# Expert weights turned in 32x32 blocks on VectorE and through DRAM, in place of TensorE transposes, with a new order on all engines

## The chip, the cores and the metric

The kernel runs on one core of a Trainium2 chip. A core has TensorE (PE, matrix products), VectorE (DVE), ScalarE (ACT), GpSimd (POOL) and SyncE (SP), which run their own instruction streams and wait for each other by semaphores. Products go from SBUF to the eight banks of PSUM, each 128 partitions by 512 fp32; DMA moves data between DRAM and SBUF and is issued here by SP and POOL. The metric is the time of one execution on the device in microseconds, lower is better.

## The reference

```
x: [8, 2048, 256] fp32, D = 256
x = x + layernorm(attention(layernorm(x)))
x = x + layernorm(ffn(layernorm(x)))

attention: q, k, v = x @ w.T ; sq, sk = elu(q) + 1, elu(k) + 1 ; per chunk of 128 rows
    A = (sq @ sk.T) * causal
    num = A @ v + sq @ S_kv ; den = A.sum(-1) + sq @ z
    S_kv += sk.T @ v ; z += sk.sum(0)          # carried from chunk to chunk of a sequence
    local = num / max(den, eps) ; memory part = (sq @ memory) / max(sq @ memory_norm, eps)
    output = (g * memory part + (1 - g) * local) @ w_o.T

ffn (hidden x, 4 heads, 1024 experts, 8 chosen a head):
    sim of x @ W_q.T with keys -> top 8 of 16 and of 64 keys -> sums of pairs -> top 8 of them
    w = silu((x . down_embed[expert]) * softmax(scores))
    experts = sum over heads and experts of w * up_embed[expert]
    dense = silu(x @ W_up.T) @ W_down.T         # 1024 wide
    out = dense + experts
```

## The kernel before

The 8 x 2048 rows are 128 tiles of 128 rows; tile t is chunk t // 8 of sequence t % 8, so a tile's state comes from the tile 8 earlier. `pipeline(body)` runs 128 + 8 - 1 steps, and in a step each engine's `body` works on several tiles: t[0] is the newest, t[7] the oldest, t[k] being the tile k behind. `if t[k] is not None` leaves out what lies before the first or past the last tile. The order of the instructions in a `body` is written out by hand or by a planner, engine by engine; engines take them strictly in that order, TensorE apart, which may load weights ahead. `steady` marks steps in the middle where some waits are left out since others imply them.

All products are fp32; the trace has two matmul passes for each `matmul`, and one for each transpose. A tile's way is as follows. x_in is loaded (SP, L360) and normalised to xn1, which TensorE turns (L516) into `t_ps`, ScalarE copying it to xn1T. Products give q and k (wqT, wkT into bank 1), v (wvo), then scores (`sig` by `sig`, L511 by `product`), the part of the state, the memory part (mem_x, bank 2), the masked scores by v (L547, bank 3), and the state's addition (L563, into banks 1 and 2, added on VectorE). The result is mixed and normalised on ScalarE, VectorE and GpSimd (power for the reciprocal root, L387) to x_mid, normalised to xn2, and turned on TensorE to xn2T.

The second half is dense over all 1024 experts. `route` gives the key scores, `deT` (two products of 512 columns, banks 6 and 7) the product of x with every down_embed. GpSimd adds every pair of keys for each head (`sums`, L401, 128x1024), VectorE takes maxima (`top`, `best`), masks (`picked`, 128x1024) and multiplies with ScalarE's exponentials (`prob`), and ScalarE's Silu writes the weights of head h to wexp[:, h, :]. Two accumulating DMAs on GpSimd's queue add the four heads: first heads 0 and 2 to 1 and 3 (L441, 1 MB), then 1 to 3 (L409, 512 KB).

The summed weights wexp[:, 3, :] have rows of the tile on the partitions, while the product with `ue` needs experts there. TensorE therefore transposes eight 128x128 blocks into banks 5 and 3 (`g_ps`, L587 and L591), and ScalarE copies each bank to gT (L692, L703). TensorE then adds two chains of eight products into bank 4: wdownT with hT (the dense part; hT is ScalarE's Silu of the wupT products, L647 and L682, in banks 2 and 1), and ue with gT:

```
product(y_ps, IC, lambda c: hT[:, t[6] % 2, c, :], lambda c: wdownT[:, c, :], stop=False)
...
pe.wait_ge(s_expert_weights_T_0_ready, t[6] + 1)
pe.wait_ge(s_expert_weights_T_1_ready, t[6] + 1)
product(y_ps, EC, lambda c: gT[:, t[6] % 2, c, :], lambda c: ue[:, c, :], start=False)
```

ScalarE copies the result, VectorE scales it and adds x_mid (L793), and SP stores it (L355). SP issues nothing else in a step but the load of x_in.

## Time and profile before

| | |
|---|---|
| median of 3 runs | 3050.55 us (3050.07 to 3052.66) |
| profiled execution | 3049.49 us, its span 3047.8 us |
| TensorE busy | 3001.7 us, 98% |
| ScalarE busy | 2622.7 us, 86% |
| VectorE busy | 2169.6 us, 71% |
| GpSimd busy | 1821.7 us, 60% |

The busy share says how much of the span an engine executed something, not whether it set the time. A timeline lists instructions in order of their start, runs of the same kind merged (x8 is eight of them), with the duration from the first start to the last end. Instructions of one engine overlap in their pipelines, so the next row often starts before the row above has ended. A note in square brackets gives idle time ahead of a row and who ended it.

### The profile page before, as it was taken

What the parts mean: (1) busy time and instruction counts of PE and PEld (TensorE: products, weight loads), DVE (VectorE), ACT (ScalarE), POOL (GpSimd) and SP (SyncE); (2) the same over time, 40 slices, a digit from 0 to 9 for tenths busy, and PEclk for the clock granted to TensorE, in tenths of its full rate; (3) what the DMA queues carried; (4) which work ended last, traced back from release to release, by engine and by line L of the source; (5) the groups of instructions that cost most, each with busy time, mean ns of one, the idle gap of its engine ahead of it and who ended that gap; (6) DMA issues with size and microseconds to landing.
All of it is one profiled execution on the core that took longest, in us unless ns stands there. A gap on an engine that the chain in (4) does not pass through costs nothing.

```text
span 3047.8 us, 48454 instructions
## 1 busy us (share of the span) xinstructions
PE 3001.7 (98%) x16426; PEld 2446.1 (80%) x16426; DVE 2169.6 (71%) x5636; ACT 2622.7 (86%) x4106; POOL 1821.7 (60%) x2455
## 2 busy tenths in 40 slices
PE   6999999999999999999999999999999999999997
PEld 5788888888888888888888888888888888888886
DVE  4777777767776777777677767776777777677774
ACT  4988888888888888888888888888888888888985
POOL 2665665566566656655665666566556655665664
PEclk8999999999999999999999999999999999999999
DMA  3443444344334434443444344334434443443443
GB/s 92 81 85 73 81 83 80 77 82 83 75 77 86 81 74 79 85 80 75 81 83 78 77 84 83 74 77 87 81 73 80 83 80 77 81 83 76 82 85 71
DMA packets 96202, 244.17 MB, mean 80 GB/s; under 512 B 8659, under 2 KB 46548, under 8 KB 95956
## 3 DMA queue, kind: packets, MB, share of 16 engines
q0 software_dynamic: 53248, 201.34, 36.7%
q1 hardware_dynamic: 42708, 39.73, 4.4%
q8 instruction: 132, 2.16, 0.3%
q14 instruction: 114, 0.93, 0.1%
HBM read 22.94 MB, written 16.78 MB: 13 GB/s over the span
## 4 chain that ended last, share of the span: by engine, by line
PE 96%; DMA 1%; issue 1%; ACT 0%; POOL 0%; DVE 0%; SPq 0%; POOLq 0%; DVEq 0%
PE banks L511 84%; PE banks L563 3%; PE banks L516 2%; PE banks L547 2%; PE banks L587 2%; PE banks L591 2%; PE banks L550 1%; DMA wexp<-wexp 1%; DMA sums<-in_L_ffn_keys_dram 0%; SPq L345 0%; POOL sums L401 0%; PE banks L502 0%; PE banks L495 0%; PE banks L480 0%; DVE prob L861 0%
## 5 line engine op out<-in xcount | busy, mean ns | idle before, releaser
L401 POOL TENSOR_TENSOR sums<-scores 128x1024 f32<-128x1024 f32 x512 | 1076.6, 2218 | 392.8 <-ACT scores L636 392.8
L511 PEld LDWEIGHTS banks<-xn2T,wupT 128*128 128x128 f32 x4096 | 477.3, 192 | 9.2 <-DVE state L848 2.7
L511 PE MATMUL banks<-deT,xn2T 128*128 128x512 f32 x1024 | 481.3, 592 | 0.0
L511 PE MATMUL banks<-xn2T,wupT 128*128 128x128 f32 x4096 | 478.2, 275 | 1.9 <-DVE state L848 1.9
L511 PE MATMUL banks<-wdownT,hT 128*128 128x256 f32 x2048 | 464.4, 380 | 0.0
L511 PE MATMUL banks<-ue,gT 128*128 128x256 f32 x2048 | 462.9, 379 | 0.0
L511 PEld LDWEIGHTS banks<-wdownT,hT 128*128 128x128 f32 x2048 | 390.1, 191 | 53.7 <-issue 0.5
L511 PEld LDWEIGHTS banks<-ue,gT 128*128 128x128 f32 x2048 | 388.6, 190 | 53.8 <-issue 0.7
L387 POOL TENSOR_TENSOR rstd<-var_eps,minus_half 128x1 f32<-128x1 f32 x512 | 329.9, 704 | 56.3 <-DVE var_eps L829 38.2
L413 POOL TENSOR_TENSOR cprob<-cmask,cdif 128x112 f32<-128x112 f32 x128 | 65.9, 515 | 396.6 <-DVE cmask L751 396.6
L511 PEld LDWEIGHTS banks<-deT,xn2T 128*128 128x128 f32 x1024 | 185.3, 190 | 129.9 <-issue 122.9
L424 POOL TENSOR_TENSOR wexp<-wexp,w_last 128x1 f32<-128x1 f32 x128 | 26.2, 205 | 364.7 <-ACT z_last L696 364.7
L511 PE MATMUL banks<-route,xn2T 128*128 128x512 f32 x512 | 242.2, 596 | 0.7 <-ACT xn2T L700 0.7
L804 DVE SCALAR_TENSOR_TENSOR sig<-banks,rqk 128x512 f32<-128x512 f32 x128 | 88.5, 691 | 193.9 <-ACT banks L642 193.9
L843 DVE SCALAR_TENSOR_TENSOR picked<-sums,cand_best,banks 128x1024 f32<-128x1024 f32 x128 | 163.9, 1280 | 62.0 <-PE banks L511 62.0
L654 ACT COPY sk_nat<-banks 128x256 f32<-128x256 f32 x120 | 44.6, 372 | 176.1 <-PE banks L550 176.1
L820 DVE TENSOR_SCALAR dens<-banks 128x2 f32<-128x2 f32 x128 | 20.5, 160 | 246.6 <-PE banks L547 246.6
L788 DVE SCALAR_TENSOR_TENSOR prob<-picked,rz,prob 128x1024 f32<-128x1024 f32 x128 | 164.5, 1285 | 13.7 <-DVE picked L784 0.5
L682 ACT ACT_TABLE_LOAD x128 | 164.2, 1283 | 2.3
L650 ACT ACT_TABLE_LOAD x127 | 162.9, 1283 | 2.2
L861 DVE SCALAR_TENSOR_TENSOR prob<-picked,rz,prob 128x1024 f32<-128x1024 f32 x128 | 164.3, 1284 | 0.0
L776 DVE SCALAR_TENSOR_TENSOR prob<-picked,rz,prob 128x1024 f32<-128x1024 f32 x128 | 163.9, 1281 | 0.0
(140 smaller groups left out, 7244.3 us busy)
## 6 DMA issues: line engine op xcount, KB each, us to landing
wexp<-wexp POOLq DMA_DIRECT2D x128, 1024.0 KB, 7.9
wexp<-wexp POOLq DMA_DIRECT2D x128, 512.0 KB, 4.7
x_in<-_attn_hidden_states_dram SPq DMA_DIRECT2D x128, 128.0 KB, 2.1
out_dram<-x_out SPq DMA_DIRECT2D x128, 128.0 KB, 1.7
wexp<-in_L_ffn_W_up_dram SPq DMA_DIRECT2D x1, 1024.0 KB, 7.1
prob<-in_L_ffn_down_embed_dram SPq DMA_DIRECT2D x1, 1024.0 KB, 9.6
ue<-in_L_ffn_up_embed_dram SPq DMA_DIRECT2D x1, 1024.0 KB, 12.0
wexp<-in_L_ffn_W_down_dram SPq DMA_DIRECT2D x1, 1024.0 KB, 13.0
```

The costliest lines, as they stand in the source:

```text
L387: return nc.gpsimd.tensor_tensor(rstd[:, n, m:m + 1], var_eps[:, n, m:m + 1], minus_half[:, :], ALU.pow)
L401: return nc.gpsimd.tensor_tensor(sums[:, k, :, :], scores[:, k, 0:XIN].unsqueeze(2).broadcast_to([P, XIN, NKEYS]), scores[:, HEADS + k, :] ...
L413: nc.gpsimd.tensor_tensor(cprob[:, :, :], cmask[:, :, :], cdif[:, :, 0:NCAND], ALU.mult).then_inc(s_cand_prob_ready, 1)
L511: last = nc.tensor.matmul(out, lhs(c), rhs(c), start=(start and c == 0), stop=(stop and c == chunks - 1))
L563: last = nc.tensor.matmul(ds_ps[:, c, :], sk_nat[:, c * P:(c + 1) * P], v_one[:, :], start=True, stop=True)
L650: nc.scalar.activation(cdif[:, :, :], cdif[:, :, :], ACT.Exp).then_inc(s_cand_exp_ready, 1)
L682: nc.scalar.activation(flat(hT[:, t[4] % 2, 4:8, :]), u_ps[1][:, :], ACT.Silu).then_inc(s_hidden_1_ready, 1)
L776: nc.vector.scalar_tensor_tensor(prob[:, 1, :], picked[:, 1, :], rz[:, t[5] % 2, 1:2], prob[:, 1, :], ALU.mult, ALU.mult).then_inc(s_head_ ...
L788: nc.vector.scalar_tensor_tensor(prob[:, 3, :], picked[:, 1, :], rz[:, t[5] % 2, 3:4], prob[:, 3, :], ALU.mult, ALU.mult).then_inc(s_head_ ...
L804: nc.vector.scalar_tensor_tensor(sig[:, t[3] % 2, :, :], eqk, 1.0, rqk[:, :, :], ALU.min, ALU.add).then_inc(s_sigma_ready, 1)
L843: nc.vector.scalar_tensor_tensor(picked[:, 0, :], head(sums, 0), best[:, 0, TOP - 1:TOP], down, ALU.is_ge, ALU.mult).then_inc(s_head_0_sel ...
L861: nc.vector.scalar_tensor_tensor(prob[:, 0, :], picked[:, 0, :], rz[:, t[4] % 2, 0:1], prob[:, 0, :], ALU.mult, ALU.mult).then_inc(s_head_ ...
```

## The change

The transposes on TensorE (L587, L591), their two copies on ScalarE and their four semaphores go. In their place VectorE turns the 32x32 blocks of the summed weights into `w_blocks`, one instruction with a write in steps of 8 elements; SP stores `w_blocks` to the DRAM scratch `w_way` (512 KB, 2 buffers), waits for that store, and issues four loads of 128 KB into gT, one for each quarter of its partitions. gT is now [128, row of the tile, chunk], and the product takes `gT[:, t[7] % 2, :, c]`, whose elements stand 8 apart.

```
-        gT = sb("gT", [P, 2, EC, P])
+        gT = sb("gT", [P, 2, P, EC])
+        w_blocks = sb("w_blocks", [P, EXPERTS])
+        w_way = nc.dram_tensor("w_way", [2, P, EXPERTS], fp32).ap()
-    SLOTS = 4
+    SLOTS = 8
+    MID_SLOTS = 8
-        STAGES = 8
+        STAGES = 10
...
+            def gather(dst, way, s_in):
+                for j in range(BLOCKS):
+                    sp.dma_start(dst[j * BLOCK:(j + 1) * BLOCK, :, :].rearrange("p (i t) c -> p i (t c)", t=BLOCK),
+                                 way.rearrange("(i q) (j n) -> j q i n", q=BLOCK, j=BLOCKS)[j]).then_inc(s_in, 16)
...
+                if t[7] is not None:
+                    sp.wait_ge(s_expert_weights_blocks_turned, t[7] + 1)
+                    sp.dma_start(w_way[t[7] % 2, :, :], w_blocks[:, :]).then_inc(s_expert_weights_blocks_out[t[7] % 2], 16)
+                    moved(sp, s_expert_weights_blocks_out, t[7], 1)
+                    gather(gT[:, t[7] % 2, :, :], w_way[t[7] % 2, :, :], s_expert_weights_blocks_in[t[7] % 2])
...
-                if t[5] is not None:
-                    pe.wait_ge(s_heads_summed, 16 * (t[5] + 1))
-                    for k in range(4):
-                        e = k
-                        last = nc.tensor.transpose(g_ps[0][:, k * P:(k + 1) * P], wexp[:, HEADS - 1, e * P:(e + 1) * P], ident[:, :])
-                    last.then_inc(s_expert_weights_T_0_in_psum, 1)
...
+                if t[7] is not None:
+                    moved(pe, s_expert_weights_blocks_in, t[7], BLOCKS)
+                    product(y_ps, EC, lambda c: gT[:, t[7] % 2, :, c], lambda c: ue[:, c, :], start=False).then_inc(s_y_in_psum, 1)
...
-                if t[5] is not None:
-                    act.wait_ge(s_expert_weights_T_0_in_psum, t[5] + 1)
-                    nc.scalar.copy(flat(gT[:, t[5] % 2, 0:4, :]), g_ps[0][:, :]).then_inc(s_expert_weights_T_0_ready, 1)
...
+            def blocks(x):
+                return x.rearrange("p (c j q) -> p j c q", j=BLOCKS, q=BLOCK)
+            def turned_blocks(x, chunks):
+                return x[:, :].rearrange("p (j t c) -> p j c t", j=BLOCKS, c=chunks)
...
+                if t[7] is not None:
+                    dve.wait_ge(s_heads_summed, 16 * (t[7] + 1))
+                    moved(dve, s_expert_weights_blocks_out, t[7] - 1, 1)
+                    nc.vector.transpose(turned_blocks(w_blocks, EC), blocks(wexp[:, HEADS - 1, :])).then_inc(s_expert_weights_blocks_turned, 1)
```

`moved` waits for the DMAs of tile t on one of two semaphores, by t's parity. x_in and x_mid now have 8 buffers each. The bodies of all engines stand in another order, and most pieces belong to a tile one or two steps older (10 stages). The three places below show it.

TensorE from the products of ue to the turn of xn2 and on to route; before:

```order
L511 MATMUL banks<-ue,gT 128x256 x7
L511 MATMUL banks<-xn2T,wupT 128x128 [waits state_ready]
L511 MATMUL banks<-xn2T,wupT 128x128 x15
L587 MATMUL banks<-ident,wexp 128x128 [waits heads_summed]
L587 MATMUL banks<-ident,wexp 128x128 x3
L591 MATMUL banks<-ident,wexp 128x128 x4
L516 MATMUL banks<-ident,xn 128x128 [waits xn2_ready,xn1T_ready]
L516 MATMUL banks<-ident,xn 128x128
L511 MATMUL banks<-xn1T,wqT 128x128 [waits hidden_1_ready,xn1T_ready]
L511 MATMUL banks<-xn1T,wqT 128x128 x3
L511 MATMUL banks<-xn1T,wkT 128x128 x4
L511 MATMUL banks<-route,xn2T 128x512 [waits xn2T_ready]
```

and with the change:

```order
L529 MATMUL banks<-xn2T,wupT 128x128 [waits state_ready]
L529 MATMUL banks<-xn2T,wupT 128x128 x7
L529 MATMUL banks<-wvo,xn1T 128x256 [waits xn1T_ready]
L529 MATMUL banks<-wvo,xn1T 128x256
L529 MATMUL banks<-xn1T,wqT 128x128 [waits hidden_1_ready]
L529 MATMUL banks<-xn1T,wqT 128x128 x3
L529 MATMUL banks<-xn1T,wkT 128x128 x4
L529 MATMUL banks<-xn2T,wupT 128x128 x8
L529 MATMUL banks<-ue,gT 128x256 [waits expert_weights_blocks_in_0]
L529 MATMUL banks<-ue,gT 128x256 x7
L534 MATMUL banks<-ident,xn 128x128 [waits xn2_ready]
L534 MATMUL banks<-ident,xn 128x128
```

The transposes of wexp are gone. The upper wupT half (into bank 1) now stands only the two wvo products ahead of wqT, which writes bank 1 again and waits for hidden_1_ready, ScalarE's hT.

ScalarE around that hT (table loads are the switches between the exponential and Silu); before, from the exponentials on:

```order
L669 ACTIVATE prob<-sums,neg_max 128x1024 [waits head_2_sums_ready]
L671 ACTIVATE prob<-sums,neg_max 128x1024 [waits head_3_sums_ready]
L676 COPY y_sb<-banks 128x256 [waits y_in_psum]
L679 COPY xn1T<-banks 128x256 [waits xn1T_in_psum]
L682 ACT_TABLE_LOAD
L682 ACTIVATE hT<-banks 128x512 [waits up_1_in_psum]
L685 ACTIVATE wexp<-prob 128x1024 [waits head_0_weighed,head_pairs_summed]
```

and with the change:

```order
L677 ACTIVATE cdif<-cdif 128x144 [waits differences_ready]
L680 ACTIVATE prob<-sums,neg_max 128x1024 [waits neg_max_ready,head_0_sums_ready]
L683 ACTIVATE mix_sq,var_eps<-mix 128x257 [waits mix_ready]
L689 ACTIVATE prob<-sums,neg_max 128x1024 [waits head_1_sums_ready]
L692 COPY xn1T<-banks 128x256 [waits xn1T_in_psum]
L695 ACT_TABLE_LOAD
L695 ACTIVATE hT<-banks 128x512 [waits up_1_in_psum]
L698 COPY v_one<-banks 128x256 [waits v_in_psum]
L701 ACT_TABLE_LOAD
L701 ACTIVATE prob<-sums,neg_max 128x1024 [waits head_3_sums_ready]
```

hT stood between exponentials and a series of Silus; now it is a single Silu between exponentials, with a table load on either side. The table load itself has no wait. A step has four table loads as before.

VectorE ahead of the maxima of the key scores; before:

```order
L780 SCALAR_TENSOR_TENSOR prob<-picked,rz,prob 128x1024 [waits head_2_selected,head_2_prob_ready]
L784 SCALAR_TENSOR_TENSOR picked<-sums,cand_best,banks 128x1024 [waits head_1_weighed,head_3_sums_ready]
L788 SCALAR_TENSOR_TENSOR prob<-picked,rz,prob 128x1024 [waits head_3_selected,head_3_prob_ready]
L793 SCALAR_TENSOR_TENSOR x_out<-y_sb,rstd,x_mid 128x256 [waits y_rstd,x_stored]
L798 MAX top<-scores 128x8 [waits route_scores_ready]
```

and with the change:

```order
L753 TENSOR_SCALAR xn<-x_mid,mv,rstd 128x256 [waits x_mid_rstd]
L769 SCALAR_TENSOR_TENSOR x_out<-y_sb,rstd,x_mid 128x256 [waits y_rstd,x_stored]
L774 SCALAR_TENSOR_TENSOR prob<-picked,rz,prob 128x1024 [waits head_3_selected,head_3_prob_ready]
L778 SCALAR_TENSOR_TENSOR prob<-picked,rz,prob 128x1024 [waits head_2_selected,head_2_prob_ready]
L783 STREAM_TRANSPOSE w_blocks<-wexp 128x4x8x32 [waits expert_weights_blocks_out_1,heads_summed]
L787 MAX top<-scores 128x8 [waits route_scores_ready]
```

The block transpose stands between the last head's product and the first of twelve maxima. It waits for the second accumulating DMA and for the store of the tile before.

## Rows read from the trace of the kernel before

**Rows 1.** The page: busy times, and TensorE's granted clock in 40 slices.

```profile
PE 3001.7 (98%) x16426; PEld 2446.1 (80%) x16426; DVE 2169.6 (71%) x5636; ACT 2622.7 (86%) x4106; POOL 1821.7 (60%) x2455
...
PEclk8999999999999999999999999999999999999999
```

**Rows 2.** PE's waits, the first row: line, releaser, total us, times, longest.

```profile
PE banks L587 <- DMA wexp<-wexp: 13.4, 3, 10.5
```

**Rows 3.** PE's timeline, one step: start, us, line, out<-in, form, count.

```profile
1500.77 0.60 PE L547 MATMUL banks<-v_one,at 128*128 128x258 f32 x2
...
1501.42 1.88 PE L511 MATMUL banks<-deT,xn2T 128*128 128x512 f32 x4
...
1504.23 3.62 PE L511 MATMUL banks<-ue,gT 128*128 128x256 f32 x16
1507.68 3.73 PE L511 MATMUL banks<-xn2T,wupT 128*128 128x128 f32 x32
1511.26 0.60 PE L587 MATMUL banks<-ident,wexp 128*128 128x128 f32 x4
...
1512.13 0.38 PE L516 MATMUL banks<-ident,xn 128*128 128x128 f32 x2
...
1514.13 1.88 PE L511 MATMUL banks<-route,xn2T 128*128 128x512 f32 x4
1515.85 1.03 PE L511 MATMUL banks<-wvo,xn1T 128*128 128x256 f32 x4
1516.72 3.62 PE L511 MATMUL banks<-wdownT,hT 128*128 128x256 f32 x16
...
1524.08 0.60 PE L547 MATMUL banks<-v_one,at 128*128 128x258 f32 x2
```

**Rows 4.** ACT's timeline in that step, same columns, idle time ahead in brackets.

```profile
1501.62 0.37 ACT L654 COPY sk_nat<-banks 128x256 f32<-128x256 f32 x1 [1.50 <-PE banks L550]
...
1505.77 1.14 ACT L671 ACTIVATE prob<-sums,neg_max 128x1024 f32<-128x1024 f32 x1
...
1508.55 1.28 ACT L682 ACT_TABLE_LOAD   x1
1509.84 0.60 ACT L682 ACTIVATE hT<-banks 128x512 f32<-128x512 f32 x1
...
1516.05 0.58 ACT L636 COPY scores<-banks 128x512 f32<-128x512 f32 x1
```

**Rows 5.** Timeline of ACT and PE where PE had waited, near the end.

```profile
2995.71 0.36 ACT L700 COPY xn2T<-banks 128x256 f32<-128x256 f32 x1
...
2996.12 1.98 PE L511 MATMUL banks<-route,xn2T 128*128 128x512 f32 x4 [0.66 <-ACT xn2T L700]
2997.95 3.62 PE L511 MATMUL banks<-wdownT,hT 128*128 128x256 f32 x16
```

**Rows 6.** POOL's timeline in the step of rows 3 and 4.

```profile
1516.71 1.90 POOL L401 TENSOR_TENSOR sums<-scores 128x1024 f32<-128x1024 f32 x1 [3.03 <-ACT scores L636]
1518.58 1.02 POOL L434 TENSOR_TENSOR cand_best<-top 128x64 f32<-128x64 f32 x4
...
1522.20 0.86 POOL L445 TENSOR_TENSOR cdif<-cand_best 128x144 f32<-128x144 f32 x1
1522.59 0.63 POOL L447 TENSOR_TENSOR neg_max<-zero,cand_best 128x4 f32<-128x4 f32 x1
```

**Rows 7.** DVE's timeline, one instruction over 1024 elements.

```profile
1506.79 1.28 DVE L861 SCALAR_TENSOR_TENSOR prob<-picked,rz,prob 128x1024 f32<-128x1024 f32 x1
```

**Rows 8.** DMA issues: out<-in, queue, count, KB each, us from issue to landing.

```profile
wexp<-wexp POOLq DMA_DIRECT2D x128, 1024.0 KB, 7.9
wexp<-wexp POOLq DMA_DIRECT2D x128, 512.0 KB, 4.7
...
out_dram<-x_out SPq DMA_DIRECT2D x128, 128.0 KB, 1.7
```

**Rows 9.** Groups by line: weight loads, busy us and mean ns, then idle.

```profile
L511 PEld LDWEIGHTS banks<-ue,gT 128*128 128x128 f32 x2048 | 388.6, 190 | 53.8 <-issue 0.7 <-ACT mix L656 0.2
```

More of the change, by code:

```diff
@@ L41, in sandwich_kernel @@
     HALF = 512
+    BLOCK = 32
+    BLOCKS = P // BLOCK
     LAST_IN = EXPERTS - 1
@@ L521, in body @@
             def body(t, steady):
+                if t[5] is not None:
+                    product(d_ps[0], DC, lambda c: xn2T[:, t[5] % 2, c, :], lambda c: deT[:, c, 0:HALF]).then_inc(s_down_0_in_psum, 1)
+                if t[4] is not None:
+                    wait(pe, s_sk_ready, t[4] + 1, KEPT)
+                    pe.wait_ge(s_mix_memory_part, t[4] + 1)
+                    if t[4] < KEPT:
+                        for c in range(DC):
+                            last = nc.tensor.matmul(ds_ps[:, c, :], sk_nat[:, c * P:(c + 1) * P], v_one[:, :], start=True, stop=True)
+                        last.then_inc(s_state_add_in_psum, 1)
@@ new lines, in body @@
+                if t[3] is not None:
+                    pe.wait_ge(s_xn1_ready, t[3] + 1)
+                    turn(t_ps, xn1).then_inc(s_xn1T_in_psum, 1)
+                if t[7] is not None:
+                    pe.wait_ge(s_hidden_1_ready, t[7] + 1)
+                    pe.wait_ge(s_hidden_0_ready, t[7] + 1)
+                    if not steady:
+                        wait(pe, s_y_ready, t[7])
+                    product(y_ps, IC, lambda c: hT[:, t[7] % 2, c, :], lambda c: wdownT[:, c, :], stop=False).then_inc(s_y_hidden_in_psum, 1)
@@ new lines, in body @@
+                if t[5] is not None:
+                    wait(pe, s_state_ready, t[5] + 2, KEPT)
+                    for k in range(4):
+                        ic = 4 + k
+                        last = product(u_ps[1][:, k * P:(k + 1) * P], DC, lambda c: wupT[:, c, ic * P:(ic + 1) * P],
+                                       lambda c: xn2T[:, t[5] % 2, c, :])
+                    last.then_inc(s_up_1_in_psum, 1)
+                if t[3] is not None:
+                    pe.wait_ge(s_xn1T_ready, t[3] + 1)
+                    product(v_ps, DC, lambda c: xn1T[:, c, :], lambda c: wvo[:, c, :]).then_inc(s_v_in_psum, 1)
+                    wait(pe, s_hidden_1_ready, t[3] - 1)
+                    if not steady:
+                        wait(pe, s_state_ready, t[3], KEPT)
+                    for side, w in enumerate((wqT, wkT)):
+                        for ec in range(DC):
+                            col = (side * DC + ec) * P
+                            last = product(qk_ps[:, col:col + P], DC, lambda c: w[:, c, ec * P:(ec + 1) * P], lambda c: xn1T[:, c, :])
+                    last.then_inc(s_qk_in_psum, 1)
@@ L593, in body @@
[L593 to L604 removed]
+                    product(d_ps[1], DC, lambda c: xn2T[:, t[4] % 2, c, :], lambda c: deT[:, c, HALF:]).then_inc(s_down_1_in_psum, 1)
@@ new lines, in body @@
+                if t[4] is not None:
+                    wait(act, s_sk_in_psum, t[4] + 1, KEPT)
+                    if t[4] < KEPT:
+                        nc.scalar.copy(sk_nat[:, :], sk_ps).then_inc(s_sk_ready, 1)
+                if t[6] is not None:
+                    act.wait_ge(s_head_3_weighed, t[6] + 1)
+                    wait(act, s_expert_weights_blocks_turned, t[6])
+                    nc.scalar.activation(wexp[:, 3, :], prob[:, 3, :], ACT.Silu).then_inc(s_head_3_weights_ready, 1)
@@ new lines, in body @@
+                if t[5] is not None:
+                    act.wait_ge(s_head_1_sums_ready, t[5] + 1)
+                    if not steady:
+                        wait(act, s_head_1_weights_ready, t[5])
+                    nc.scalar.activation(prob[:, 1, :], head(sums, 1), ACT.Exp, bias=neg_max[:, t[5] % 2, 1:2]).then_inc(s_head_1_prob_ready, 1)
+                if t[3] is not None:
+                    act.wait_ge(s_xn1T_in_psum, t[3] + 1)
+                    nc.scalar.copy(flat(xn1T), t_ps).then_inc(s_xn1T_ready, 1)
@@ L701, in body @@
[L701 to L706 removed]
+                    act.wait_ge(s_head_2_sums_ready, t[5] + 1)
@@ L708, in _ @@
+                    nc.scalar.activation(prob[:, 2, :], head(sums, 2), ACT.Exp, bias=neg_max[:, t[5] % 2, 2:3]).then_inc(s_head_2_prob_ready, 1)
             pipeline(body)
@@ L790, in body @@
[L790 to L796 removed]
+                    dve.wait_ge(s_x_mid_rstd, t[5] + 1)
```

470 lines of the change are left out of this document (200 added, 270 removed).

## The prediction

> **What bounds the kernel now.** I read the page's busy shares first. TensorE is busy for 98% of the span at full granted clock [rows 1], so nothing speeds the kernel up unless TensorE gets less work, and anything that makes TensorE wait costs in full. The waits of PE then say when it is idle: the longest entry in all is 13.4 us in 3 waits for the summed expert weights, at start and end of the program [rows 2]. In between there are none. TensorE's timeline of one step shows this: the product of the masked scores (L547) starts at 1500.77 and again at 1524.08, a period of **23.31 us**, with no idle note in between [rows 3]. 128 tiles x 23.31 = 2983.7, and the span is 3047.8, so 64.1 us is set-up, filling and draining. The reader is to use starts, not durations, in that timeline: a row's duration includes the drain of the pipeline, and what a group costs is the distance to the next start. The other engines have room: VectorE is busy 71%, ScalarE 86%, GpSimd 60% [rows 1], or 16.6, 20.0 and 13.9 us of 23.3.
>
> **What leaves TensorE.** The eight transposes of a tile's expert weights (L587, L591) start at 1511.26, and the next group starts at 1512.13 [rows 3]: 0.87 us a tile, 111.4 us over 128 tiles. (The 0.60 us durations would say 1.2 a tile; that counts the drain twice.) All other products stay, so the new floor is 23.31 - 0.87 = **22.44 us** a step. ScalarE loses two 512-column copies (some 0.5 us each between starts), which is no gain in itself since it isn't the bound.
>
> **What the rest adds.** I laid the new order of one step end to end with the distances of before: 0.112 us for a 128-column pass (3.58 us for 32 from 1507.68), 0.216 for 256 columns (3.45 for 16 from 1504.23), 0.43 for 512 (1.72 for 4, from 1514.13), and 0.22 for a pair of transposes (a quarter of 0.87) [rows 3]. Zero is the first down product (deT). Then the state product starts at 1.72, xn1's turn at 2.59, wdownT at 2.81, the upper half of wupT at 6.26, wvo at 8.05, wqT and wkT at 8.92, the lower half of wupT at 10.70, ue with gT at 12.49, xn2's turn at 15.94, route at 17.04 (over at 18.76), the last product at 22.01. Each wait is then checked against its producer.
>
> (a) *The one that is late: hT between wupT and wqT.* Both products use bank 1. ScalarE must empty the upper wupT half (Silu, 0.60 us [rows 4]) before wqT writes there, and only wvo (0.87 us, 1515.85 to 1516.72 [rows 3]) now lies in between. ScalarE starts 0.20 us after a group on TensorE is over (sk_nat at 1501.62; its transposes are over where deT starts, 1501.42 [rows 3, 4]). TensorE starts 0.05 after a ScalarE result (xn2T from 2995.71 for 0.36, route at 2996.12), and such a resumed group takes 0.11 longer (1.83 us to the next start, not 1.72), since its weight load could not run ahead [rows 5]. 0.20 + 0.60 + 0.05 + 0.11 - 0.87 = **0.09 us**; I take 0.10 a step, 12.8 us. It lies between 0, if the 0.11 is hidden, and 0.3. A table load precedes this Silu, but stands ahead of the wait, so it is not in the sum as long as ScalarE arrives early. Does it?
>
> (b) *ScalarE before that.* From the end of route: scores copied from +0.20 on, key sums from +0.86 (0.66 later, as 1516.05 to 1516.71), then on GpSimd 1.87 for the sums (1516.71 to 1518.58), 1.02 for the candidates, 1.87 for the next sums, cdif at +5.6, 0.39 later (1522.20 to 1522.59) the small add to wexp, for which I allow 0.39 too, and neg_max (0.63) ready by +7.0 [rows 4, 6]. ScalarE then has two exponentials (1.14 each, about 1.0 between starts), a square and a copy (0.4 each) and a table load (1.28): 4.2 us, so it is ready for hT at +11.2 [rows 4]. TensorE finishes the upper wupT half at 3.68 + 8.05 = +11.7 after the end of route, and ScalarE could start at +11.9. 0.7 us of slack, so no loss; but the chain crosses three engines.
>
> (c) *VectorE's block transpose.* The trace has none. It moves 1024 elements per partition; every 1024-element instruction here takes 1.28 us [rows 7], whose ends with a strided write could be 1 and 4 times that, 1.2 to 4.8. I take 1.3, as the next row does. Its place is between the product for head 2 (over at about 17.2 in my layout) and the 12 maxima of the next tile (scores there at 19.6), 2.4 us; the candidates need the maxima 0.56 us later still, and the mask that TensorE wants at 22.01 leaves 0.7. So up to about 3 us is **free**, and VectorE's total of 16.6 + 1.3 fits in 22.4. A page gives a price: the Trainium skill, "VectorE: DVE Perf Modes", section "The three transpose paths", has 311 ns on VectorE for a 128x128 bf16 block against 390 on TensorE, and advises TensorE where PSUM will do as destination. By that the estimate is eight times 311, 2.5 us: still free.
>
> (d) *The way through DRAM.* 512 KB out, then four times 128 KB back, on SP. The 512 KB accumulating move takes 4.7 us and the 128 KB store 1.7 [rows 8]; so 1.7 to 4.7 for the store and, with four issues of about 0.4, 3 to 5 for the loads: at most 10 us. The blocks are turned by 18.5 and wanted at 12.49 of the next step, 34.9: 16 us. Free. SP is held during the store, and behind it wait only the x load (now 8 buffers deep) and the x store, whose buffer is wanted a step later. The new traffic can overlap the 1 MB pair sum on GpSimd's queue (7.9 us [rows 8]), issued at about 2.6 and wanted at 11.6, for which that leaves 1.1 us. Behind it GpSimd makes xn2's rstd (13.7); TensorE wants xn2 at 15.94, 1.8 us of slack. Free, unless the sum is slowed by 3 us.
>
> (e) *Weights read in steps of 32 bytes.* gT is now [128, tile row, chunk], so each of the 16 weight loads for ue picks every eighth element. No load in the trace is strided. A load shows 190 ns under products 216 apart [rows 9]; under wupT the products, each with its load, are 112 apart [rows 3], so a load really needs no more than 112. Bounds: nothing, or twice the row, 380 ns, which adds 164 x 16 = 2.6 us a step. I take nothing: at twice 112 = 224 it costs 8 ns a load, 0.13 us a step.
>
> (f) *Two more stages*, 137 steps and not 135. The work is the same; only idle time at the ends grows. At the end the last tile needs about 1.3 + 4 + 4 us for turning and the way through DRAM in place of the 0.87 + 0.6 for transposes and copy, while the wdownT product (3.45, longer at a lower clock), now issued ahead of the wait, leaves the tail: +4. At the start the first products for ue come later, behind work of four tiles: 0 to 10. Together **+6**, from 2 to 20.
>
> **Sum.** The profiled execution took 3049.5. 3049.5 - 111.4 + 12.8 + 6 = 2956.9; the median of before is 1.1 above it: **2958**. The main case runs from 2941 (no stall at wqT, ends +2) to 2984 (stall 0.3 a step).
>
> **Rivals.**
> *Another loop is late.* By (b) and (c) the slacks on the other engines are 0.4 to 2 us, from distances in another order. If ScalarE or VectorE reaches one of these places 0.3 to 0.8 us late each step, 38 to 102 us come on top: 2995 to 3060. For it: the chain of three engines in (b), and mix's memory part, which by my layout leaves ScalarE 0.5 us before TensorE wants it. Against: VectorE and ScalarE keep 4.5 and 3 us of idle time a step to catch up with.
> *Strided weight loads, slower.* If a load takes 380 ns, the 16 products of ue go at that distance: +2.6 x 128 = +336, **3294**. It decides from about 260 ns a load on (0.72 us a step). For it: 190 ns in the rows is near 216. Against: 112 under wupT. The Trainium skill has a rule that speaks for it: "SBUF — State Buffer" (section "The DMA port swizzle", its note on cachelines) says that SBUF has 16-byte lines, that every access to a new line pays, and that fp32 may step four elements for free; here the step is eight. It doesn't say how much it pays, and no run here shows it yet.
> *The block transpose is slow, slower.* At 4.8 us it is 1.8 over its 3 us: the maxima, the candidates and the mask come late, +230, 3188. It decides at about 3.7 us. Only the strided write speaks for it.
> *The change doesn't do what it says*: excluded by the order, where TensorE's rows L587 and L591 are gone, and ScalarE still loads four tables a step.
>
> **Chances.** Main case 0.62 (faster). Another loop 0.18: 0.13 faster, 0.02 within, 0.03 slower. Strided loads 0.14 slower. Slow transpose 0.06, of which nearly all is slower. 0.2% of 3050 is 6 us, about what a measurement tells from no change. Faster 0.75, same 0.03, slower 0.22. The range takes in the main case with 9 us below it for an error in my reading of distances, and the other loop nearly whole, and leaves the two slow cases out: 2932 to 3052.
>
> **What would show it.** TensorE's timeline with a period near 22.54 us; one wait per step at wqT for ScalarE's hT of 0.1 us and no other; the products of ue 216 ns apart (rival: 380); VectorE's transpose below 3 us and no wait of the maxima's users; DRAM loads landed before TensorE asks, so no DMA among PE's waits except at the ends. I am wrong if PE waits for anything else in the steady part, or if the ends grew by more than 20 us.

## The result and the profile after

The changed kernel takes **3029.7 us** (median of 4 runs, 3024.5 to 3034.5) against 3050.3 for the kernel before in the same comparison (4 runs, 3050.0 to 3052.7): a ratio of 0.993, 95% interval 0.9915 to 0.9945. It is faster, as forecast, but by 21 us where 92 were forecast. 3029.7 lies inside the range of 2932 to 3052 and well outside the main case of 2941 to 2984. That it lies in the range is luck: the range reached so far up for a rival that didn't occur ("another loop is late"); see "Why the prediction was off".

The profiled execution is the slowest of the four: 3034.5 us, with a span of 3032.7. From its page, the busy times (PEld is TensorE's weight loads) and the granted clock in tenths of full speed:

```profile
PE 2970.0 (98%) x15402; PEld 2431.6 (80%) x15402; DVE 2420.2 (80%) x5764; ACT 2532.4 (84%) x3854; POOL 1955.8 (64%) x2455
...
PEclk8999999999999999999999999999999999999998
```

The clock is full but at the two ends, as before [rows 1]. TensorE has 1024 instructions fewer than in [rows 1], as it must (128 x 8), and is still busy for 98% of the span. It bounds this kernel too. Its busy time fell by 31.7 us, from 3001.7 to 2970.0, where the transposes alone should have taken away 111.4. So something on TensorE itself got longer. One step shows what, first ScalarE's part at hT and then TensorE's (start, us, operation, and in brackets idle time before):

```profile
1521.38 0.60 ACT L695 ACTIVATE hT<-banks 128x512 f32<-128x512 f32 x1 [1.25 <-PE banks L529]
```

```profile
1519.39 1.95 PE L529 MATMUL banks<-xn2T,wupT 128*128 128x128 f32 x16
1521.18 1.03 PE L529 MATMUL banks<-wvo,xn1T 128*128 128x256 f32 x4
1522.05 1.14 PE L529 MATMUL banks<-xn1T,wqT 128*128 128x128 f32 x8
1523.03 1.06 PE L529 MATMUL banks<-xn1T,wkT 128*128 128x128 f32 x8
1523.92 1.95 PE L529 MATMUL banks<-xn2T,wupT 128*128 128x128 f32 x16
1525.70 4.11 PE L529 MATMUL banks<-ue,gT 128*128 128x256 f32 x16
1529.65 0.38 PE L534 MATMUL banks<-ident,xn 128*128 128x128 f32 x2
...
1545.06 1.14 PE L529 MATMUL banks<-xn1T,wqT 128*128 128x128 f32 x8
```

The kernel before has for the two groups on the bank of hT

```profile
1512.35 1.06 PE L511 MATMUL banks<-xn1T,wqT 128*128 128x128 f32 x8
1513.24 1.06 PE L511 MATMUL banks<-xn1T,wkT 128*128 128x128 f32 x8
```

Read the starts. From wqT at 1522.05 to the next wqT at 1545.06 the period is **23.01 us**, and it is the same over the whole steady part; 22.54 was forecast and 23.31 was the old one [rows 3]. Every distance is as before but two:

- wqT to wkT is 0.98 and was 0.89: +0.09, the wait for hT. The bank is full at 1521.18, ScalarE starts its Silu at 1521.38 and ends at 1521.98, and wqT follows.
- ue with gT takes from 1525.70 to 1529.65, 3.95, and took 3.45 [rows 3]: **+0.50 us**, with no idle note. That was forecast at nothing.

22.44 + 0.09 + 0.50 = 23.03, against 23.01 measured. The distance of 3.95 is that of this step; in most steps it is 3.94, against 3.45 or 3.46 before, so the term is 0.48 to 0.50.

The groups by line (busy us, mean ns of one, idle before) put the second on the weight loads, and give the duration of the block transpose; behind them come rows of the DMA issues (KB each, us from issue to landing):

```profile
L529 PEld LDWEIGHTS banks<-ue,gT 128*128 128x128 f32 x2048 | 502.7, 336 | 16.1 <-DMA gT<-w_way 14.5
...
L529 PEld LDWEIGHTS banks<-wdownT,hT 128*128 128x128 f32 x2048 | 380.5, 191 | 54.2 <-issue 7.5
...
L783 DVE STREAM_TRANSPOSE w_blocks<-wexp 128x1024 f32<-128x1024 f32 x128 | 260.9, 2039 | 4.8 <-DMA wexp<-wexp 4.6
...
w_way<-w_blocks SPq DMA_DIRECT2D x128, 512.0 KB, 2.6
gT<-w_way SPq DMA_DIRECT2D x512, 128.0 KB, 3.0
```

The 2048 loads of gT last 336 ns each, those of hT 191, as all did before [rows 9]. Only gT is read with a step, of eight elements.

PE's waits (total us, times, longest) show that nothing else is late in the steady part, since no entry that names an engine or a DMA has more than eight waits, but for hT's:

```profile
PE banks L529 <- DMA gT<-w_way: 13.7, 2, 8.6
...
PE banks L529 <- ACT xn2T L639: 4.6, 8, 0.8
...
PEld banks L529 <- ACT hT L695: 28.9, 126, 0.6
```

(The PEld row is the weight loader's, which counts from the moment it could have run ahead; what it costs TensorE is the 0.09 of the starts.) The two waits for gT lie at the end, in TensorE's timeline of the last tiles:

```profile
2993.28 5.37 PE L529 MATMUL banks<-wdownT,hT 128*128 128x256 f32 x16 [5.49 <-ACT y_sb L650]
3007.27 5.42 PE L529 MATMUL banks<-ue,gT 128*128 128x256 f32 x16 [8.62 <-DMA gT<-w_way]
...
3021.99 6.43 PE L529 MATMUL banks<-ue,gT 128*128 128x256 f32 x16 [5.06 <-DMA gT<-w_way]
```

Here every us of the new way counts, because there is hardly any other work left. The wdownT product, 3.62 us long elsewhere [rows 5], lasts 5.37 in the first row, after an idle stretch. Over the last 57.7 us (time, then busy us of PE, PEld, DVE, ACT and POOL, granted clock, DMA share and GB/s) the view by windows says

```profile
2975.00:3032.70 57.70, 33.69 (x133) 27.94 (x131) 20.08 (x35) 20.19 (x30) 15.80 (x22) 0.81 0.49 119
```

a granted clock of 0.81 and 33.7 us of work, where the kernel before has 0.91 and 39.7 in its last 57.8.

**The account.** Before's span is 3047.8, after's 3032.7, a difference of -15.1:

| term | us | from |
|---|---|---|
| transposes gone | -111.4 | 0.87 x 128 |
| strided loads of gT | +64.0 | 0.50 x 128 |
| wait for hT | +11.5 | 0.09 x 128 |
| TensorE idle | +16.6 | span less busy: 46.1 before, 62.7 after |
| left over | +4.2 | not resolved; with 0.48 for the loads it is +6.8; the lower clock at the ends is in it |

Idle time and the rest are at the ends. 128 periods leave 64.1 us of before's span and 3032.7 - 2945.3 = 87.4 of after's. Both ends grew. The first wqT product starts at 42.7 us and not at 37.2; in the other runs of kernels with this opening it starts between 38.6 and 42.0, so a part of these 5.5 us is the run's and not the change's. From the last tile's wqT to the end there are 91.6 us, of which TensorE is busy 64.7 at a mean clock of 0.88; before, 74.5 us, 56.4 of them busy, at 0.93.

### The profile page after: what moved, and what is told of

Same layout as the page of the kernel before. It is cut to its first block, busy times and chain, and to the rows that moved or that the text cites. A ratio compares the mean times of both kernels' runs of the same rounds, so it can differ in the third digit from the quotient of the medians.

```text
span 3032.7 us, 46880 instructions
## 1 busy us (share of the span) xinstructions
PE 2970.0 (98%) x15402; PEld 2431.6 (80%) x15402; DVE 2420.2 (80%) x5764; ACT 2532.4 (84%) x3854; POOL 1955.8 (64%) x2455
## 4 chain that ended last, share of the span: by engine, by line
PE 95%; DMA 2%; issue 1%; DVE 1%; POOL 1%; ACT 1%; SPq 0%; POOLq 0%; DVEq 0%
PE banks L529 86%; PE banks L547 3%; PE banks L534 2%; PE banks L608 2%; PE banks L601 1%; DMA wexp<-wexp 1%; DMA sums<-in_L_ffn_keys_dram 0%; SPq L353 0%; POOL sums L418 0%; DMA gT<-w_way 0%; DVE w_blocks L783 0%; PE banks L513 0%; POOL rstd L404 0%; PE banks L520 0%; PE banks L498 0%
## 5 line engine op out<-in xcount | busy, mean ns | idle before, releaser
L418 POOL TENSOR_TENSOR sums<-scores 128x1024 f32<-128x1024 f32 x512 | 1033.9, 2019 | 749.7 <-ACT scores L653 749.7
L404 POOL TENSOR_TENSOR rstd<-var_eps,minus_half 128x1 f32<-128x1 f32 x512 | 498.0, 1110 | 69.0 <-DVE var_eps L855 35.7
L529 PE MATMUL banks<-ue,gT 128*128 128x256 f32 x2048 | 528.9, 412 | 13.7 <-DMA gT<-w_way 13.7
L529 PEld LDWEIGHTS banks<-ue,gT 128*128 128x128 f32 x2048 | 502.7, 336 | 16.1 <-DMA gT<-w_way 14.5
L783 DVE STREAM_TRANSPOSE w_blocks<-wexp 128x1024 f32<-128x1024 f32 x128 | 260.9, 2039 | 4.8 <-DMA wexp<-wexp 4.6
L811 DVE SCALAR_TENSOR_TENSOR picked<-sums,cand_best,banks 128x1024 f32<-128x1024 f32 x128 | 163.9, 1280 | 85.2 <-PE banks L529 85.0
L695 ACT ACTIVATE hT<-banks 128x512 f32<-128x512 f32 x128 | 76.4, 597 | 148.1 <-PE banks L529 148.1
L758 DVE SCALAR_TENSOR_TENSOR picked<-sums,cand_best,banks 128x1024 f32<-128x1024 f32 x128 | 163.9, 1280 | 35.5 <-POOL sums L418 35.5
L831 DVE SCALAR_TENSOR_TENSOR prob<-picked,rz,prob 128x1024 f32<-128x1024 f32 x128 | 191.2, 1494 | 0.0
L787 DVE MAX8 top<-scores 128x8 f32<-128x16 f32 x512 | 83.6, 163 | 116.5 <-ACT scores L653 116.2
L435 POOL DMA_DIRECT2D wexp<-wexp x128 | 158.4, 1237 | 27.9 <-issue 7.4
```

The source lines that it names most:

```text
L404: return nc.gpsimd.tensor_tensor(rstd[:, n, m:m + 1], var_eps[:, n, m:m + 1], minus_half[:, :], ALU.pow)
L418: return nc.gpsimd.tensor_tensor(sums[:, k, :, :], scores[:, k, 0:XIN].unsqueeze(2).broadcast_to([P, XIN, NKEYS]), scores[:, HEADS + k, :] ...
L435: pool.dma_start(wexp[:, 1::2, :], wexp[:, 0::2, :], accum_op=ALU.add).then_inc(s_head_pairs_summed, 16)
L529: last = nc.tensor.matmul(out, lhs(c), rhs(c), start=(start and c == 0), stop=(stop and c == chunks - 1))
L695: nc.scalar.activation(flat(hT[:, t[5] % 2, 4:8, :]), u_ps[1][:, :], ACT.Silu).then_inc(s_hidden_1_ready, 1)
L758: nc.vector.scalar_tensor_tensor(picked[:, 0, :], head(sums, 2), best[:, 2, TOP - 1:TOP], down, ALU.is_ge, ALU.mult).then_inc(s_head_2_sel ...
```

## The experiments

The theory: 0.50 us a step is the price of reading gT with a step of eight; 0.09 is the wait for hT; the remainder of the shortfall is at the ends; transpose and DRAM trip are otherwise hidden. The rivals were that TensorE is slowed by the new DMA traffic, that removing the transposes brought less than 0.87, and that the trip or the transpose costs something in every step. The edits stand against the changed kernel.

### Step 2 in place of 8

```
-product(y_ps, EC, lambda c: gT[:, t[7] % 2, :, c], ...)
+product(y_ps, EC, lambda c: gT[:, t[7] % 2, :, :].rearrange("p t c -> p (t c)")
+    [:, (c // 2) * 2 * P:(c // 2 + 1) * 2 * P].rearrange("p (t s) -> p t s", s=2)[:, :, c % 2], ...)
```

> As e_step4, with steps of 2 elements (8 bytes), so that two elements lie in each 16 bytes; the output again isn't the reference's for the same reason. Theory 1: 3.45 us for the ue passes, weight loads near 190 ns and not 336, period near 22.5 us. Theory 2: 3.95 us and 23.01, since the DMA traffic is the same.

Measured: 2971.5 us in one run, beside 3051.2 for the kernel before. The period is 22.53. Start, us and operation around ue, then the row of the weight loads:

```profile
1519.68 3.62 PE L529 MATMUL banks<-ue,gT 128*128 128x256 f32 x16
1523.14 0.38 PE L534 MATMUL banks<-ident,xn 128*128 128x128 f32 x2
```

```profile
L529 PEld LDWEIGHTS banks<-ue,gT 128*128 128x128 f32 x2048 | 393.4, 197 | 48.2 <-DMA gT<-w_way 11.8
```

3.46 us for the group and 197 ns a load, with the same DMAs, the same bytes and the same transposes. The step of the read is the whole of the 0.50 us, and DMA traffic none of it. 2971.5 is inside the main case of the forecast: with that one term at nothing, as it was taken, the rest of the sum holds to 15 us. A real layout that loads this cheaply has costs elsewhere, as a later run shows.

### Step 4

The same line, with 4 in place of 2.

> The changed kernel with one edit: the weights of the ue products are read from gT in steps of 4 elements (16 bytes) and not 8, all loads, stores and waits unchanged. Which element belongs to which row is thereby mixed up, so the output isn't the reference's; the work is the same in size. In the changed kernel the 16 passes of ue take 3.95 us to the next start, 0.50 more than before. Theory 1 (the step of the weight loads costs it): falls below 3.95; with a cost only beyond 16 bytes it is back at 3.45 and the period of 23.01 falls to 22.5, some 64 us in all; if every visit to another 16 bytes costs the same it stays at 3.95. Theory 2 (the new DMA traffic into gT disturbs TensorE's reads there): stays at 3.95.

Measured: 3016.4 us in one run, period 22.91.

```profile
1517.55 4.00 PE L529 MATMUL banks<-ue,gT 128*128 128x256 f32 x16
1521.39 0.38 PE L534 MATMUL banks<-ident,xn 128*128 128x128 f32 x2
```

```profile
L529 PEld LDWEIGHTS banks<-ue,gT 128*128 128x128 f32 x2048 | 489.4, 328 | 14.3 <-DMA gT<-w_way 12.7
```

3.84 for the group, 328 ns a load. A step of 16 bytes costs nearly what 32 do, 0.38 us against 0.49, and one of 8 bytes nothing between starts. Neither form of the theory as recorded fits: 3.84 is neither the 3.45 of a cost beyond 16 bytes only, nor quite the 3.95 of an equal cost for every visit. The edge lies between steps of two and four elements, and it fits that what counts is whether two neighbouring elements of the read share 16 bytes; a step of three wasn't run. The Trainium skill has two readings of this: "Advanced Engine Details and Errata", section "SBUF Cachelines", asks for at least two hits on a 16-byte line, with which these runs agree; "SBUF — State Buffer", in the note that the prediction cited, adds that fp32 may step four elements for free, and the 328 ns contradict it for weight loads. The measurement decides.

### The transposes put back, as dead work

```
+wait(pe, s_route_scores_ready, min(t[7] + 3, TILES))
+for k in range(EC):
+    nc.tensor.transpose(bank[5][:, (k % 4) * P:(k % 4 + 1) * P], ident[:, :], ident[:, :])
```

> The changed kernel with eight transposes of the identity on TensorE put back ahead of the ue products (into bank 5, nothing reads them), as work of the size that the change removed. Theory (eight transposes are worth 0.87 us a step by start distances and TensorE sets the period): period 23.01 + 0.87 = 23.88 us, +111 us, if no wait hides a part. Rival (they are worth 1.2 us as the durations say): 24.2. Rival (something other than TensorE sets the period, TensorE's busy share notwithstanding): period below 23.5.

Measured: 3131.5 us in one run. Between the upper end of the wupT product and ue now stand

```profile
1525.24 1.04 PE L585 MATMUL banks<-ident 128*128 128x128 f32 x8
1526.12 4.11 PE L529 MATMUL banks<-ue,gT 128*128 128x256 f32 x16
```

0.88 us, and the period is 23.88 or 23.89, from 23.01. Eight transposes are worth 0.87 a step in the new order too; the main gain was real, and was spent elsewhere. The span grew by 97.0 and not by the 111 expected: the steady part pays in full, but 128 periods leave 72 us of the span, 15 less than in the changed kernel. The granted clock there is higher, 0.94 from 40 to 80 us (0.87 in the changed kernel) and 0.88 in the last 57.7 (0.81). So what an end costs moves by 15 us with the work around it, which this single run can't explain further.

### The other half of wupT first

wqT waits because it is the second product after the bank that Silu must empty. Here the lower half of wupT, which uses another bank, goes between wvo and wqT:

```
+if t[5] is not None:      # 16 products of the lower wupT half, moved up from behind wkT
+    for k in range(4): ... product(u_ps[0][:, k * P:(k + 1) * P], ...)
 if t[3] is not None:      # wqT, wkT
```

> The changed kernel with the lower half of the wupT products moved up, between wvo and wqT, so that ScalarE has 1.79 us more to empty bank 1 before wqT writes it. Theory (the wait of wqT for ScalarE's hT costs 0.09 us a step): wqT to wkT goes from 0.98 to 0.89 us, the wait row for hT goes, the period from 23.01 to 22.92, 12 us in all. Rival (the wait only takes time that TensorE would lose at the next late place): period stays within 0.02 of 23.01 and another wait row grows, since q and k are now 1.79 us later for ScalarE and VectorE.

Measured: 3023.8 us (4 runs, 3022.8 to 3025.0), ratio 0.9908 (0.9892 to 0.9925).

```profile
1522.30 1.95 PE L529 MATMUL banks<-xn2T,wupT 128*128 128x128 f32 x16
1524.09 1.06 PE L529 MATMUL banks<-xn1T,wqT 128*128 128x128 f32 x8
1524.98 1.06 PE L529 MATMUL banks<-xn1T,wkT 128*128 128x128 f32 x8
```

wqT to wkT is 0.89 again and the period 22.92: the 0.09 is the wait for hT. In the medians 5.9 us came of the 11.5, and the intervals of this and the unedited kernel overlap slightly; the profiled runs differ by 9.5. The start takes some of it back: the ninth tile's wqT starts 7 us later than in the changed kernel, at a granted clock of 0.83 from 80 to 120 us, where that has 0.96.

### The block transpose twice

```
+nc.vector.transpose(turned_blocks(w_other, EC), blocks(wexp[:, HEADS - 1, :]))
 nc.vector.transpose(turned_blocks(w_blocks, EC), blocks(wexp[:, HEADS - 1, :]))...
```

> The changed kernel with VectorE's block transpose done twice, first into a buffer that nothing reads: 4.1 us and not 2.04. Theory (some 3 us at this place are free, as laid out in the prediction): period 23.01 + 1.1 = 24.1 us. Rival (the steps before the transpose can move earlier too, so VectorE's idle 20% counts): below 23.3. The other way, if only the 0.9 us that VectorE waits for the scores is free: 24.2 or more.

Measured: 3081.4 us in one run, the span 47.0 longer, for 2.04 us more of VectorE a step. Some 30 of it are in the steady part, where the mean period is 23.28, so 0.27 us a step; the rest is at the ends.

```profile
PE banks L609 <- DVE at L795: 28.1, 42, 1.9
```

More than half of the periods are unchanged (23.01 to 23.05); the others are longer, by up to 1.6. The place that gets late is the masked scores, which TensorE multiplies with v; (c) had named it as the tightest. One transpose of 2.04 is hidden with something to spare, and two, 4.08 us, exceed the room on average by 0.3. So the room is nearer 3.8 than the 3 us laid out in the prediction, and the 24.1 expected here was too high; 23.28 is the rival's (below 23.3).

### Twice through DRAM

```
+sp.dma_start(w_more[t[7] % 2, :, :], w_blocks[:, :]).then_inc(s_more[t[7] % 2], 16)
+moved(sp, s_more, t[7], 1)
```

> The changed kernel with the store to DRAM done twice (first to another scratch, waited for), so that each tile's way to gT is 2.6 to 3 us longer. Theory (the way is hidden in the steady part and paid at the end, where the last two tiles follow each other): period 23.01 unchanged, PE's waits for gT at the end grow by 3 to 6 us in all, and the total by as much. Rival (the way is already near its limit in the steady part): period above 23.05 and DMA gT among the waits of many steps.

Measured: 3044.3 us (8 runs, 3038.4 to 3045.9), ratio 0.9973 (0.9963 to 0.9983). The period stays at 23.01, but for five steps that are 0.1 to 0.6 longer. PE's wait for gT, and the longest of it in the timeline:

```profile
PE banks L533 <- DMA gT<-w_way: 23.1, 7, 10.7
```

```profile
3016.04 5.92 PE L533 MATMUL banks<-ue,gT 128*128 128x256 f32 x16 [10.70 <-DMA gT<-w_way]
```

The trip is hidden in the steady part even with another store in it, and is paid at the ends, where the waits for gT grew by 9.4 us, more than the 3 to 6 expected: three of them now fall in the last 75 us, of 4.5, 10.7 and 5.5. The medians grew by 14.5 and the profiled spans by 9.8. What the rest of the 14.5 is wasn't resolved.

### Can the 0.50 be had back? First, a layout with a step of 2

DVE turns four groups of 256 elements, and sixteen DMAs of 32 KB, not four of 128, bring gT into pairs:

```
-gT = sb("gT", [P, 2, P, EC])
+gT = sb("gT", [P, 2, 4, P, 2])
...
+for g in range(4):
+    sp.dma_start(dst[j * BLOCK:(j + 1) * BLOCK, g, :, :]..., way...[j, g]).then_inc(s_in, 16)
...
-product(y_ps, EC, lambda c: gT[:, t[7] % 2, :, c], ...)
+product(y_ps, EC, lambda c: gT[:, t[7] % 2, c // 2, :, c % 2], ...)
...
+for g in range(4):
+    last = nc.vector.transpose(out_v[:, g], in_v[:, g])
```

> The changed kernel with gT laid out so that the weight loads step 2 elements: VectorE turns the blocks in four instructions of 256 elements, the way back from DRAM is 16 loads of 32 KB with runs of 256 bytes in place of 4 of 128 KB with 1 KB. Theory (weight loads in steps of 8 bytes cost nothing, the way through DRAM is hidden): ue passes 3.46 us, period 22.52 us, 63 us less than the changed kernel, near 2966. Rival (16 issues at about 0.45 us and short runs make the way late): DMA gT shows among PE's waits in the steady part and the period stays above 22.7.

Measured: 3017.8 us (4 runs, 3015.6 to 3024.9), ratio 0.9889 (0.9874 to 0.9903). PE's wait for gT, the load and transpose groups, and SP's timeline (start, us, operation):

```profile
PE banks L530 <- DMA gT<-w_way: 46.1, 39, 12.3
```

```profile
L530 PEld LDWEIGHTS banks<-ue,gT 128*128 128x128 f32 x2048 | 395.3, 198 | 96.1 <-DMA gT<-w_way 58.2
...
L787 DVE STREAM_TRANSPOSE w_blocks<-wexp 128x256 f32<-128x256 f32 x512 | 181.8, 416 | 9.0 <-DMA wexp<-wexp 8.9
```

```profile
1513.88 11.18 SPq L364 DMA_DIRECT2D gT<-w_way  x15
```

The load is cheap (198 ns, group 3.46), and the undisturbed steps take 22.53. But in nearly a third of the steps (39 of 128) TensorE stands still for gT, and the mean period is 22.81. SP needs 11.2 us to issue fifteen of the sixteen loads; in the changed kernel the four took 1.74 (from 1511.98). The 16 us of slack that made the trip free are used up, by issuing and not by bytes.

### The same, with the wupT order of above

The edit is the two last ones together.

> As f_lay2, and with the lower wupT half ahead of wqT, as in e_up0_first. Theory (both costs are independent and TensorE alone sets the period): 22.44 us, the floor worked out from the distances of before, near 2953. Rival (with TensorE faster, a loop through another engine becomes late): period above 22.5 with a wait row per step for it.

Measured: 3040.6 us (5 runs, 3036.9 to 3044.4), ratio 0.9961 (0.9948 to 0.9974). It is slower than without the new order. TensorE asks for gT in 62 steps before it is there:

```profile
PE banks L530 <- DMA gT<-w_way: 61.2, 62, 12.5
```

The mean period is 22.95, against 22.81 with the old order. The timelines show a reason why gT is late more often. Without the wupT order VectorE's transpose starts at 1509.80 and route on TensorE at 1509.92; with it route starts at 1504.71 and the transpose at 1505.30. So the way to gT begins 0.7 us later in TensorE's step, where it had nothing to spare. That it is q and k, 1.79 us later, which push VectorE back is inferred, and that this is the whole of the 0.14 us a step is not shown.

### The same without DRAM

Sixteen moves from SBUF to SBUF, straight from w_blocks to gT; no store, no wait for it:

```
+for i in range(BLOCKS):
+    sp.dma_start(dst[j * BLOCK:(j + 1) * BLOCK, :, i * BLOCK:(i + 1) * BLOCK, :]...,
+                 way[i * BLOCK:(i + 1) * BLOCK, j * 256:(j + 1) * 256]...).then_inc(s_in, 16)
-sp.dma_start(w_way[t[7] % 2, :, :], w_blocks[:, :])...
```

> As f_lay2_up0, but without the DRAM scratch: 16 moves of 32 KB straight from w_blocks to gT, in SBUF. The steady part has room for either way, so the period should stay at 22.44. Theory (some of the longer ends come from the trip through DRAM, store 2.6 us and its wait ahead of the loads): 2 to 6 us less in all than f_lay2_up0, and shorter waits for gT in the last 50 us. Rival (the ends are long because of the stages and of the wait of the last tiles for each other, not of the trip): within 2 us.

Measured: 3034.4 us (4 runs, 3032.9 to 3034.6), ratio 0.9938 (0.9921 to 0.9954): 6.2 us less than with DRAM.

```profile
PE banks L528 <- DMA gT<-w_blocks: 55.6, 51, 12.2
```

```profile
1503.47 12.67 SPq L364 DMA_DIRECT2D gT<-w_blocks  x16
```

The store is gone and the waits stay: the mean period is 22.88 and not the 22.44 expected. The sixteen issues now last 12.9 us (median of the steps), against 10.7 with DRAM, and so use up most of the 2.6 us that the store took. What is late is the issuing, with either source.

### A dense copy on ScalarE

Four DMAs and the step of 8 stay, and ScalarE copies gT into rows of chunks before TensorE reads it; ScalarE, not TensorE, pays for the step:

```
+moved(act, s_expert_weights_blocks_in, t[7], BLOCKS)
+wait(act, s_y_in_psum, t[7])
+nc.scalar.copy(gC[:, :, :], gT[:, t[7] % 2, :, :].rearrange("p t c -> p c t")).then_inc(s_gC_ready, 1)
...
-product(y_ps, EC, lambda c: gT[:, t[7] % 2, :, c], ...)
+product(y_ps, EC, lambda c: gC[:, c, :], ...)
```

> The changed kernel with 4 loads as it has them, and one ScalarE copy (1024 elements, read in steps of 8, written densely into a new buffer gC) ahead of the hT Silu; the ue products take their weights from gC, densely. ScalarE waits 1.25 us for the wupT product just there. Theory (dense weight loads give back 0.50 us a step, and the copy of about 1.1 us fits into ScalarE's wait): ue passes 3.46 us, period 22.53, 2966 to 2970 in all. Rival (the copy takes longer than 1.25 us, and hT and so wqT come later): ue passes 3.46, but wqT waits longer by what the copy is over 1.25, and the period is above 22.6.

Measured: 3074.8 us (4 runs, 3072.8 to 3075.9), ratio 1.0075 (1.0058 to 1.0092): slower than the kernel before. The copy's row, then TensorE's timeline and one row of ScalarE's:

```profile
L698 ACT COPY gC<-gT 128x1024 f32<-128x1024 f32 x128 | 267.7, 2091 | 15.2 <-DMA gT<-w_way 15.2
```

```profile
1513.63 1.03 PE L531 MATMUL banks<-wvo,xn1T 128*128 128x256 f32 x4
1515.25 1.16 PE L531 MATMUL banks<-xn1T,wqT 128*128 128x128 f32 x8 [0.59 <-ACT hT L701]
```

```profile
1511.18 2.10 ACT L698 COPY gC<-gT 128x1024 f32<-128x1024 f32 x1
1513.30 1.28 ACT L701 ACT_TABLE_LOAD   x1
1514.60 0.60 ACT L701 ACTIVATE hT<-banks 128x512 f32<-128x512 f32 x1
```

ue is back to 3.46, but the copy stands before hT in ScalarE's program, so hT comes at 1515.2, and wqT starts 1.62 us after wvo and not 0.87. The period is 23.28. This is the spot that (b) of the prediction watched: 0.7 us of slack worked out at hT, 1.25 measured, and a copy of 2.1 us put in front of it, where some 1.1 had been expected.

### The copy, with the lower half of wupT first

> As g_copy, with the lower wupT half ahead of wqT. Theory: the wait of wqT for hT goes too, even if the copy takes up to 3 us, period 22.44 us, the floor from the distances of before; 2953 to 2960 in all. Rival (the later q and k, or the later scores copy, are late now): period above 22.5 with a wait row for it.

Measured: **2985.7 us** (4 runs, 2985.1 to 2987.7), ratio 0.9785 (0.977 to 0.9799). It beats both kernels: 66 us better than before in the same comparison, 44 better than the changed kernel.

```profile
1521.69 1.95 PE L531 MATMUL banks<-xn2T,wupT 128*128 128x128 f32 x16
1523.48 1.06 PE L531 MATMUL banks<-xn1T,wqT 128*128 128x128 f32 x8
1524.37 1.06 PE L531 MATMUL banks<-xn1T,wkT 128*128 128x128 f32 x8
1525.26 3.62 PE L531 MATMUL banks<-ue,gC 128*128 128x256 f32 x16
1528.72 0.38 PE L536 MATMUL banks<-ident,xn 128*128 128x128 f32 x2
```

```profile
PE banks L531 <- ACT gC L699: 13.1, 2, 9.8
...
PEld banks L531 <- ACT xn2T L642: 35.6, 121, 0.7
```

There are 1.79 us of TensorE work more between the bank and its next use, and wqT waits no longer; ue takes 3.46. The period is 22.56, 0.12 over the floor of 22.44, and what is left is a small wait for xn2T in nearly every step. The very copy that lost 45 us against the changed kernel wins 44 with one other group moved, a group that by itself had brought 6. At the end it waits for gC (13.1 us in 2 waits) as the changed kernel does for gT. The 2953 to 2960 expected are missed by some 30 us: 15 are the 0.12 a step, the rest is at the ends, where 128 periods leave 96 us and not 87. ScalarE is now busy for 93% of the span.

## Why the prediction was off

By the prediction's own parts:

**TensorE bounds, and eight transposes are worth 0.87 us.** Right. TensorE is at 98% before and after, and the dead transposes cost 0.87 in the new order.

**(a) The wait for hT.** Right, in mechanism, place and size: 0.09 worked out, 0.09 measured, from the same 0.20 between product and Silu (1521.18, 1521.38). Moving another product in between removes it.

**(b) ScalarE's slack.** Right for this kernel: at hT ScalarE is ready 1.25 us before the bank is full. The copy showed how little it takes to use it up.

**(c) The block transpose.** 1.3 us taken, 2.04 measured, inside the bounds; free, as said. The Trainium skill's price for a bf16 block ("VectorE: DVE Perf Modes", section "The three transpose paths") had led to an estimate of 2.5, nearer than the row I took.

**(d) The trip through DRAM.** 2.6 for the store, 3.0 for a load, and the last load issued at about 1513.7, so some 7.5 us from the transpose's end to gT where up to 10 were allowed, against 16. Free in the steady part, as the doubled store confirms. The pair sum on GpSimd's queue, which the new traffic could have slowed, lands after 8.0 us and took 7.9 before.

**(e) Weights read in steps of 32 bytes. This is the step that failed.** It was taken as nothing and costs 0.50 us a step, 64 us in all, of the 78 by which the profiled execution missed the sum. The bounds held it (0 to 2.6), but the value taken inside them rested on "a load really needs no more than 112" and on the choice that a strided one needs twice that, 224, of which all but 8 ns is hidden. The products of ue are now 3.95/16 = 247 ns apart, that is 2.2 times 112, not 2. Since a product of 256 columns covers only 216, the first doubling was nearly free, and every ns beyond it is paid 2048 times. The term stood at a threshold, and there the lower end was no neutral choice: between the 8 ns of a doubling and the 164 of the upper bound, something like the doubling's 0.13 us was the least to take, and the doubt belonged in the sum. The rival with slower strided loads had the mechanism right and the price wrong: it read 380 ns of record as distance. The record is now 336, and the distance 247.

**(f) The ends.** +6 taken, with 20 as the far bound; the ends grew by 21 (the last two terms of the account) or 23 (128 periods taken off each span), 16.6 of it TensorE's idle time. Some 5 us lie before the first wqT, partly the run's own, and 17 behind the last. There, the kernel before waited for wexp (2.7, and the 10.5 of [rows 2]). Now gT is late twice, by 8.62 and 5.06 us, with a wait of 5.49 ahead of them. The sum had priced the trip once, for the last tile, and it is paid in two tiles; that accounts for a part of the 17. How the rest divides between the lower clock (0.88 against 0.93) and the two stages wasn't resolved.

**The rivals.** Another loop being late had 0.18 and a band of 2995 to 3060, and for its sake the range went up to 3052. No loop is late in the steady part, so that 3029.7 falls into that band and into the range is chance.

Put together: 3049.5 - 111.4 + 12.8 + 6 = 2956.9 was the sum against the profiled execution. With 64 for (e), 11.5 for (a) and about 21 for (f) it is 3034.6, and 3034.5 was measured. Much of this agreement is by construction, since the terms are read from the same trace; what supports it from outside is that the step of 2, the moved wupT half and the dead transposes moved the period by 0.48, 0.09 and 0.87. The signs that the prediction set itself ("the products of ue 216 ns apart", "or if the ends grew by more than 20 us") point at the same two terms.

## What to carry to other kernels

Before work is moved off the bounding engine, look at how that engine will read the new layout: an operand written by somebody else in a convenient order may be read by it with a stride, at a price per instruction that no idle time shows and that a product only partly covers. Take a distance between starts, not a record's length, for what a load costs, and where a cost lies beside a cover of nearly the same size, put a value above the cover into the sum. A stride can be moved to an engine with room, but only together with the order of the work around it; and a longer way for a tile's data, hidden in the steady part, is paid at the end, in more than one tile if several are still in flight.
